# A post-norm decoder layer: the cross-attention's mask added by TensorE, weights by half blocks, last stages by halves

## The reference

```python
x = layernorm(x + self_attn(x))       # 32 heads of 16, qkv and output projections with biases
x = layernorm(x + cross_attn(x, ctx)) # q = x, k = v = ctx: 8 groups of 4 query heads, no projections
x = layernorm(x + ffn(x))
# cross_attn: scores = q @ k.T / 4 + mask[128, 128];  softmax(scores) @ v
# ffn: r = softmax(x @ gate_w.T)      # 8 experts
#      (x * (r @ in_scale)) @ sign(weight).T * (r @ out_scale) + bias
```

## Time and profile before

| | before |
|---|---|
| median of 3 runs | 362.21 us |
| profiled execution | 361.09 us |
| its span, first to last instruction | 359.2 us |
| mean granted TensorE clock | 0.979 |
| TensorE busy | 323.3 us (90%) |
| VectorE busy | 255.0 us (71%) |
| ScalarE busy | 190.0 us (53%) |
| GpSimd busy | 133.9 us (37%) |

### The profile page before, as it was taken

The page is one execution under the profiler, slowest core; times in us unless marked ns, Lnnn a source line. Parts: engine busy times, 40 slices in busy tenths (PEclk is TensorE's granted clock), DMA queues, the critical chain, the costliest instruction groups (busy, mean ns, idle before and its releaser), DMA issues.

```text
span 359.2 us, 7880 instructions
## 1 busy us (share of the span) xinstructions
PE 323.3 (90%) x2803; PEld 237.8 (66%) x2803; DVE 255.0 (71%) x828; ACT 190.0 (53%) x375; POOL 133.9 (37%) x217
## 2 busy tenths in 40 slices
PE   4997989897989999989999999999898997999992
PEld 3896866586765687767657698677475665754561
DVE  0693287135789955879999565989984778798646
ACT  2922733831148777531677865415689726536440
POOL 3352385973531124251472332423442243210311
PEclk9998999998999999999999999999999999899997
DMA  7946872454484012569451008982600045300001
GB/s 252 381 166 175 232 157 73 105 173 128 151 242 107 6 37 68 152 190 259 102 153 47 5 11 254 274 184 59 157 9 13 2 120 138 94 32 5 0 0 58
DMA packets 26119, 42.86 MB, mean 119 GB/s; under 512 B 7437, under 2 KB 17817, under 8 KB 23777
## 3 DMA queue, kind: packets, MB, share of 16 engines
q1 hardware_dynamic: 25769, 41.82, 41.5%
q10 hardware_dynamic: 312, 0.55, 0.4%
HBM read 29.58 MB, written 12.32 MB: 117 GB/s over the span
## 4 chain that ended last, share of the span: by engine, by line
PE 37%; DVE 34%; DMA 9%; issue 6%; SPq 4%; ACT 4%; POOL 4%; ACTq 0%; POOLq 0%; DVEq 0%
DVE x L948 7%; PE bank_a L1048 5%; DVE nma L865 4%; PE bank_a L1050 4%; PE bank_a L1049 4%; SPq L435 4%; PE bank_b L1233 3%; DMA out_dram<-x 3%; DVE wL L1017 2%; DMA ks<-scr_k 2%; DVE stb L829 2%; DVE x L965 2%; PE bank_a L1168 2%; PE bank_a L1137 2%; PE bank_a L1062 2%
## 5 line engine op out<-in xcount | busy, mean ns | idle before, releaser
L948 DVE CUSTOM_DVE_ANT_0 x<-bank_b,mraw 128x128 bf16<-128x128 f32 x192 | 42.3, 285 | 2.2 <-DMA out_dram<-x 1.5
L865 DVE TENSOR_REDUCE nma<-bank_a 128x4 f32<-128x512 f32 x64 | 40.0, 681 | 1.5 <-PE bank_a L1137 1.3
L741 ACT ACTIVATE pa<-bank_a 128x512 f32<-128x512 f32 x64 | 35.9, 598 | 8.7 <-PE bank_a L1154 6.8
L1048 PE MATMUL bank_a<-xH,wH 128*128 128x256 f32 x128 | 37.7, 294 | 0.7 <-DVE wL L1017 0.7
L1049 PE MATMUL bank_a<-xL,wH 128*128 128x256 f32 x128 | 36.5, 285 | 0.0
L1050 PE MATMUL bank_a<-xH,wL 128*128 128x256 f32 x128 | 36.5, 285 | 0.0
L606 POOL TENSOR_TENSOR qkp<-qr,qkp 128x512 bf16<-128x512 f32 x16 | 18.8, 1178 | 41.2 <-DVE qkp L861 41.2
L749 ACT ACTIVATE pb<-bank_b 128x512 f32<-128x512 f32 x54 | 29.9, 600 | 7.6 <-PE bank_b L1224 3.7
L712 ACT ACTIVATE qkp<-bank_a,bqk 128x256 bf16<-128x256 f32 x32 | 13.3, 471 | 33.9 <-PE bank_a L1050 23.8
L856 DVE SCALAR_TENSOR_TENSOR qr<-bank_a,bqk,qkp 128x256 f32<-128x256 f32 x32 | 14.0, 478 | 22.2 <-ACT qkp L712 22.1
L585 POOL TENSOR_SCALAR rsb<-mvb 128x1 f32<-128x1 f32 x16 | 3.7, 234 | 68.0 <-DVE mvb L831 68.0
(11 more groups left out here) (211 smaller groups left out, 808.4 us busy)
## 6 DMA issues: line engine op xcount, KB each, us to landing
wraw<-in_L_attn_attn_qkvw_dram SPq DMA_DIRECT2D x3, 1024.0 KB, 9.5
scr_q<-qkp SPq DMA_DIRECT2D x8, 384.0 KB, 3.0
qs<-scr_q SPq DMA_DIRECT2D x8, 384.0 KB, 4.5
scr_k<-qkp SPq DMA_DIRECT2D x8, 384.0 KB, 3.0
ks<-scr_k SPq DMA_DIRECT2D x8, 384.0 KB, 6.4
scr_x<-xp SPq DMA_DIRECT2D x8, 384.0 KB, 2.8
qx<-scr_x SPq DMA_DIRECT2D x8, 384.0 KB, 4.3
qs<-scr_q SPq DMA_DIRECT2D x8, 256.0 KB, 4.7
```

Source lines behind the costliest of these rows:

```text
L741: act.activation(pa[:, n % NP, :], pa_bank(i, *step)[:], ACT.Exp, scale=HD ** -0.5).then_inc(*ra.is_empty(i, *step))
L865: dve.tensor_reduce(nma[:, b, 4 * j:4 * j + 4], pa_bank(i, *step)[:].rearrange("p (m t) -> p m t", m=KT), AX.X, ALU.max, negate=True).then ...
L948: last = dve.tensor_tensor_reduce(unread[:, part * P:(part + 1) * P], pb_bank(i, *step)[:, r * P:(r + 1) * P], mraw[:], -1.0, -LOWEST, ALU ...
L1048: pe.matmul(dst, lh, rh, start=kt == 0, stop=False)
```

## The change

1. *Mask.* In every group TensorE adds the mask to `s`: two f32r products of 512 columns, the identity by the mask's high part and by its low part, laid down four times side by side. In group 3 it does the same for `st`, with mask and identity exchanged; the steps `sm`, and `sd` of group 3, are gone. In groups 0 to 2 `sd` stays with ScalarE. VectorE's maxima are the plain ones, one instruction a unit, in every group; x2 is no longer a scratch, and its wait for the stored output stands at `ot:b,0`. The raw mask lies in a part of `pa` until it is split.
2. *Weights.* The query block comes in four transfers; step `w` goes by five pieces, two halves of the query block, two of the key block, the value block; VectorE takes 2, 3, 3, 3 and 2 of the four tiles of each, GpSimd the others. A query or key step waits for its own pieces. The warming transposes before the first products change from 14, 8 and 30 to 0, 24 and 20, and x is transposed before the small operands.
3. *Router.* The exponentials are transposed as they are; the square of their sum's reciprocal is applied to the product's result, in the instruction that scales it. The scales are plain f32, 8 rows, and step `scales` is gone.
4. *Norm after the cross-attention.* After `ot:b,0` GpSimd adds the residual of the first 256 columns; VectorE takes the statistics of each half.
5. *Group 3's last stages.* `cx`, `is`, `ff`, `n2`, `n3` and the store go by halves of 256 columns.
6. *Buffers.* `rc` (context split) shares `xr` (x split), with waits between the two.
7. The table has an order of its own, and `UNREAD` 72 fillers in 21 places where it had 158 in 58.

```diff
@@ SyncE
-            sp.dma_start(wraw[:, :, 0:H], wv[:, :, 0:H]).then_inc(ld_w[0], 16)
+            for kt in range(KT):
+                sp.dma_start(wraw[:, kt, 0:H], wv[:, kt, 0:H]).then_inc(ld_wq[kt], 16)
...
@@ GpSimd
+                elif thread == "B" and name == "ot" and step[2] == 0:
...
+                    b = step[1]
+                    rb.wait_emptied(pool, i, *step)
+                    pool.tensor_tensor(by_head(x2[:, b, :])[:, 0:2], by_head(x2[:, b, :])[:, 0:2], tile_permuted(x1[:, b, :])[:, 0:2], ALU.add).then_inc(half_sum[b], 1)
...
@@ VectorE
+                    for k in range(GB):
+                        if earlier("ctx", k, place):
+                            dve.wait_ge(c_third[k], earlier("ctx", k, place))
                     rest = xr[:]
...
-                    if rb.has_mask(i, *step):
+                    if rb.has_mask(i, *step) or i in ADDED:
                         dve.tensor_reduce(nmb[:, b, :].rearrange("p (h k) -> p h k", k=KT)[:, 4 * (g % 2):4 * (g % 2) + 4, g // 2],
...
+                    if u == 1:
+                        dve.wait_ge(half_sum[b], 2 * i + 1)
+                        dve.bn_stats(stb[:, b, 0], x2[:, b, 0:HALF]).then_inc(half_sum[b], 1)
...
-                        dve.tensor_tensor(by_head(x2[:, b, :]), by_head(x2[:, b, :]), tile_permuted(x1[:, b, :]), ALU.add).then_inc(ln_b[b], 1)
-                        deviations(2 * i, x2[:, b, :], b)
+                        dve.tensor_tensor(by_head(x2[:, b, :])[:, 2:4], by_head(x2[:, b, :])[:, 2:4], tile_permuted(x1[:, b, :])[:, 2:4], ALU.add).then_inc(ln_b[b], 1)
+                        dve.wait_ge(ln_b[b], 6 * i + 1)
+                        dve.bn_stats(stb[:, b, 1], x2[:, b, HALF:]).then_inc(ln_b[b], 1)
+                        dve.wait_ge(half_sum[b], 2 * i + 2)
+                        aggregate(2 * i, b)
...
+                    dve.tensor_tensor(rl[:, b:b + 1], sl[:, b:b + 1], sl[:, b:b + 1], ALU.mult).then_inc(route_made[b], 1)
+                    dve.wait_ge(route_made[b], 2 * i + 1)
+                    dve.reciprocal(rl2[:, b:b + 1], rl[:, b:b + 1]).then_inc(route_made[b], 1)
...
+                    if i == LAST:
+                        h = step[2]
+                        part = slice(h * HALF, (h + 1) * HALF)
+                        rb.wait_full(dve, i, *step)
+                        dve.scalar_tensor_tensor(scaled[:, part], pb_bank(i, *step)[:, 0:HALF], rl2[:, b:b + 1], scaled[:, part],
+                                                 ALU.mult, ALU.mult).then_inc(*rb.is_empty(i, *step))
...
-                    for kt in range(KT if blk == 1 else WSPLIT):
+                    for kt in range(LOWS[piece]):
...
@@ TensorE
                     fresh = not rb.has_mask(i, *step)
+                    if fresh and i in ADDED:
+                        fresh = False
+                        if i == 0:
+                            pe.wait_ge(masks, 2)
+                        d4 = dst[:].rearrange("p (r t) -> p r t", r=4)
+                        for part in (mH, mL):
+                            pe.matmul(d4, idr[:], part[:].rearrange("p (o t) -> p o t", o=1).broadcast_to([P, 4, P]),
+                                      start=part is mH, stop=False, skip_group_check=True)
...
+                    if not rb.has_mask(i, *step):
...
+                        ident4 = idr[:].rearrange("p (o t) -> p o t", o=1).broadcast_to([P, 4, P])
+                        pe.matmul(d4, mH[:], ident4, start=True, stop=False, skip_group_check=True)
+                        pe.matmul(d4, mL[:], ident4, start=False, stop=False, skip_group_check=True)
...
-                    pe.wait_ge(route_made[b], i + 1)
-                    pe.transpose(dst[0:4 * E, 0:P], rts[:, b].rearrange("p k e -> p (k e)"), idf[:]).then_inc(*rb.is_full(i, *step))
+                    rb.wait_emptied(pe, i, "rt", b)
+                    pe.transpose(dst[0:E, 0:P], el[:, b, :], idf[:]).then_inc(*rb.is_full(i, *step))
...
@@ ORDER, start, before and after (group 3's end: cx, is, ff by halves)
-    C0.small A0.xt:0 A0.xt:1 C0.w:0 C0.w:1 A0.lc C0.w:2 A0.q:0 A0.q:1 A0.ldq:0 A0.q:2 A0.q:3 A0.ldq:1 A0.v:0 A0.ldk:0
+    C0.w:0 A0.xt:0 A0.xt:1 C0.small C0.vs A0.lc B0.cp:0 C0.w:1 C0.w:2 C0.w:3 C0.w:4 A0.q:0 A0.q:1 A0.ldq:0 A0.v:1
+    A0.q:2 A0.q:3 A0.ldk:0 A0.v:0 A1.xt:0 A1.xt:1 A0.ldk:1 A0.ldq:1 C0.ow B0.ctx:0 C0.mask A1.q:0 A1.q:1 A0.s:0,0
...
```

More of the change, by code:

```diff
@@ L58 @@
[L58 to L67, removed]
@@ L675, in _ @@
+                elif thread == "C" and name == "w":
+                    piece = step[1]
+                    for kt in range(LOWS[piece], KT):
+                        pool.wait_ge(w_high, KT * piece + kt + 1)
+                        low, raw = w_views(wL, wraw, kt, piece)
+                        pool.tensor_tensor(low, raw, high_view(kt, piece), ALU.subtract).then_inc(w_low_p, 1)
                 elif thread == "C" and name == "ow":
@@ L919, in _ @@
                         dve.wait_ge(c_third[1], i)
+                    for k in range(GB):
+                        if earlier("xt", k, place):
+                            dve.wait_ge(b_third[k], earlier("xt", k, place))
                     dve.tensor_tensor(rc[:], pb_bank(i, *step)[:, 0:P], cp[:, b, 0, :], ALU.subtract).then_inc(*rb.is_empty(i, *step))
@@ L1236, in _ @@
                     b = step[1]
-                    pe.wait_ge(x2_made[b], i + 1)
-                    for kt in range(KT):
-                        last = quarter(dst, kt, x2[:, b, kt * P:(kt + 1) * P])
+                    pe.wait_ge(x2_made[b], i + 1 + sum(step[2:]))
+                    for k, kt in enumerate(tiles_of(i, step)):
+                        last = quarter(dst, k, x2[:, b, kt * P:(kt + 1) * P])
                     last.then_inc(*rb.is_full(i, *step))
@@ L1259, in _ @@
                     rb.wait_emptied(pe, i, "rr", b)
-                    for kt in range(KT):
-                        last = pe.matmul(dst[:, kt * P:(kt + 1) * P], icS[:, kt * P:(kt + 1) * P], rT[:, tokens(b)], start=kt == 0, stop=kt == KT - 1,
+                    if i == 0 and b == 0:
+                        pe.wait_ge(ld_cs, 32)
+                    for k, kt in enumerate(tiles_of(i, step)):
+                        last = pe.matmul(dst[:, k * P:(k + 1) * P], icf[:, kt * P:(kt + 1) * P], rT[:, tokens(b)], start=k == 0, stop=True,
                                          skip_group_check=True)
@@ L1277, in _ @@
                     dst = pb_bank(i, "small")
-                    for _ in range(14):
-                        pe.transpose(dst[:, 0:P], idf[:], idf[:])
                     pe.wait_ge(ld_small, 48)
```

361 lines of the change are left out of this document (200 added, 161 removed), and 19 rows, old and new, of the table UNREAD.

## The result

The changed kernel takes 373.48 us (median of 4 runs, 370.54 to 377.0) against 362.17 (361.53 to 362.82) before: ratio 1.0285, 95% interval 1.0192 to 1.0378, so slower, and beyond the upper end of the range, 364 us. A second set of runs of the same kernel, beside the experiments, gave 374.7 us and 1.0346 (1.0292 to 1.0399), the whole interval more than 2% above the kernel before. Ratios leave out runs that are longer at a lower granted clock (one of the four above, two of ten of the f32r scales, 405.75 and 517.17 us, seven of ten of the mask's high part, one each of the last two kernels), while medians and ranges hold every run. here are those of the changed kernel unless another is named.

The account below looks back on a forecast made before the run. The middle alternates between TensorE and VectorE. Head -4.5, middle +2.0, last scores -3.3, last stages -4.6 sum to -10.4 from 361.09: 350.7, median 351.8, stated as 351.5 us; own range 345 to 358, 8-in-10 range 339 to 364.

Parts of the forecast that it names:

- Router and scales: Router: four small VectorE steps leave the last stages' path, 1.0 us; plain f32 scales no change, upper bound 1.7 us.
- third rival: Router's scale products: plain f32 takes four passes, 6.9 us, about 60% on the path, giving 356 us; chance 0.03.
- Mask in the middle: Groups 0 to 2: TensorE gets 22.5 us, 12.4 on the path; VectorE's shorter maxima give back 6.5 us.
- first rival: Middle: TensorE becomes the bound, 85% of the added 22.5 us on the path, giving 368 us; chance 0.19.
- Head: Kernel start: split weights, earlier x transposes and reordered reload bring first scores earlier, gain 4.5 us.
- head gain absorbed: Head's gain is lost before the cross-attention, by key 1 or the output projection's weights: 356 us; chance 0.12.
- Last group's scores: Group 3: TensorE adds the mask, 16 VectorE copies go; stretch from 24.8 to 21.5 us, gain 3.3.
- Last stages by halves: From the last values step to the end, 23.8 us: working by halves gains 4.6 us, between 2.5 and 6.
- Residual by halves: Groups 0 to 2: half the residual sum goes to GpSimd, gain 2.9 us; VectorE's added wait taken as 0.
- Scratch in x2 and shared buffers: Moved wait for the output's store: nothing, at most 0.44 us; shared split buffers: 0, up to 0.6 us in 8 places.

Follow-up runs that it names:

- the last two kernels: Both repairs, bf16 mask, last mask on VectorE, mask's step moved, 32-row f32r whole scales: 384.2 us; whole scales on both repairs and moved step only: 374.03 us.
- both repairs: Changed kernel with f32r scale products in one pass and only the mask's high part ahead of the maxima: 357.23 us, ratio 0.9837.

## Why the prediction was wrong

*Router and scales: the step that failed worst.* "I take no change, upper bound 0.11 x 16 = 1.7 us". With one f32r pass in its place the changed kernel takes 11.3 us less; plain f32 alone costs 6 to 7 in the old order. The reading was at fault: I held the time of one instruction of the plain f32 row against one f32r product. That row counts 8 for a step of four products, two instructions to a product, and I had the row in hand. The third rival had the mechanism, 6.9 us of TensorE and a chance of 0.03; measured are 9 at the full clock and 10.8 in all. The rule I had set aside holds: the Trainium skill ("FP8 and Floating Point Precision", TensorE Precision Notes) gives true FP32 four passes. The trace agrees: 1.05 us for 512 columns is 4.5 of the filler's slots of 0.234.

The other half of that step is four VectorE instructions that go from between the exponential and its transpose. I gave that 1.0 us, in the last stages only. In the kernel before, TensorE waited for them for 2.0 us over the whole span, four times, 0.8 the longest; in the changed kernel 0.2 us are left, for ScalarE's exponential. So this term was about right for the old order. Where two such instructions return to the new order, the wait is 11.4 us: the new order has no room for them. Rounding the weights once keeps that wait away without the price of plain f32, at the precision of one f32r pass.

*Mask in the middle.* "0.468 us by the filler's slot" was 0.55: the first product of a pair starts 0.314 us before the second, the second 0.238 before the scores, as the rows of one unit show:

```profile
266.08 0.48 PE L1272 MATMUL bank_b<-mH,idr 128*128 128x512 f32 x1
266.40 0.40 PE L1272 MATMUL bank_b<-mL,idr 128*128 128x512 f32 x1
266.64 0.40 PE L1275 MATMUL bank_b<-kx,qx 96*128 96x128 bf16 x4
266.84 0.48 PE L1272 MATMUL bank_b<-mH,idr 128*128 128x512 f32 x1
```

The filler's 0.234 was f32r behind f32r; behind bf16 scores the first costs 0.08 more. The unit is 0.76 us (266.08 to 266.84), not 0.69, while a plain maximum is the 0.60 I had. Over 48 units that is 4 us. The larger error is the net price: in the old order alone the move costs 14 us where I had 12.4 - 6.5 = 5.9. If VectorE gave back the 6.5, then 80% of TensorE's 26 us was on the path and not 55%; no run separates the two. The first rival ("TensorE becomes the bound", 0.19) was the case that came, and the time came out above its 368 us. The reason that I gave against it did not hold: I counted the run-outs of its bursts as room, and the second stretch shows 75.57 of 76 us busy. B0.s:0,0 to B2.st:1,7 grew by 11.3 us; with f32r scales it still grew by 7.4, with both repairs by 1.4.

*Head.* The first score was forecast near 44.5 and stands at 45.04: the weights' halves and the reordered reload did about what the sum said. Of these 4.0 us, 0.6 are left at A0.st:0,0 and 3.0 at B0.s:0,0, so "head gain absorbed" (0.12) came in small part, 1.5 us short of the sum's 4.5, and by another place than the two I named. What I didn't price is the splitting of the mask: its two VectorE instructions of 1.5 us stand in the new table ahead of group 1's query parts, and these ahead of the first maxima. The first maximum starts at 48.87, 0.6 us earlier than before; moving that one step won 3.7 us at B0.s:0,0 and 3.8 at the end. The eight fillers behind it (53.13, 2.11 us) held VectorE up once, for 1.25 us; no run prices them.

*Last group's scores.* I began the stretch a unit too early: 310.57 is the last unit of the first sequence, and the second's first is at 312.45, so before it was 22.9 us and not 24.8. After, it is 322.60 (the mask's first product) to 346.43, 23.8 us in place of 21.5. The eight score units take 6.0 for 5.5. A transposed unit behind another takes 0.70 (329.19 to 329.89), as in the sum, but one in front of a values step or a transpose about 0.88, so the sixteen are 11.9 for 11.0; the four values steps take 4.05 for 3.6, and the transposes, with a wait of 0.34 in the last, 1.8 for 1.4. No single term is far off: the 3.3 us of gain were 1.9 of the wrong start, and what is left was less than the 2.3 by which the terms were short.

*Last stages by halves.* Forecast -4.6 from the end of the last values step to the end (23.8 us before); measured 26.6, +2.8. With f32r scales it is 21.7 (340.11 to 361.82), -2.1: the right sign, and just under the 2.5 to 6 of the sum. The difference of 4.9 us is the plain f32 products and the lower clock, in the changed kernel's tail:

```profile
358.13 1.22 PE L1332 MATMUL bank_a<-rT,icf 8*128 8x128 f32 x4
359.14 1.06 PE L1332 MATMUL bank_b<-rT,icf 8*128 8x128 f32 x4
359.99 1.91 PE L1336 MATMUL bank_b<-ocf,rT 8*128 8x512 f32 x2
361.83 1.22 PE L1344 MATMUL bank_b<-swT,zH 128*128 128x256 f32 x4
```

3.7 us for one sequence's scales. The stretch around it, below the one before it:

```profile
348.00:356.00 8.00, 7.83 (x49) 4.63 (x47) 4.81 (x17) 2.90 (x11) 2.50 (x4) 1.00 0.01 2
356.00:366.00 10.00, 10.00 (x39) 8.01 (x39) 4.71 (x13) 2.17 (x5) 0.22 (x1) 0.52 0.00 1
```

The granted clock is 0.52, the lower of the two levels (1.2 of 2.4 GHz), after 8 us in which TensorE was busy for 7.83 at the full one. I took 0 for that and kept up to 4 us; TensorE is busy for all of these 10 us, so by my estimate, from the clock of 0.52 alone, up to 5 of them are the clock's. With f32r scales the granted clock from 341 us to the end is 0.91.

*Residual by halves.* VectorE waits for GpSimd's half three times, 3.0 us, 1.0 the longest, within what the range held for it:

```profile
DVE stb L988 <- POOL x L657: 3.0, 3, 1.0
```

*Scratch in x2 and shared buffers* leave no wait in the lists of the changed kernel worth a term.

In one sum, by stretches of the profile against the forecast's -10.4: the head -3.0 for -4.5; from B0.s:0,0 to B3.st:1,7, which is the middle and most of the last scores, +15.1 for -1.3; from there to the end +1.7 for -4.6. By causes, undone one on top of the other: 374.7 us, 363.44 with f32r scales (11.3 less), 357.23 with the mask's high part alone (6.2 less), 353.41 with the mask's step moved (3.8 less). What the mask's move costs in the new order no run isolates; in the old one it is 14 us. With three small edits the kernel takes 3.0% less than before, at one f32r pass for the scales and the rounded mask under the maxima. That this is 2 us from the forecast is luck: the forecast had both mask products, and its terms for the middle, the last scores and the last stages are off one by one.

## What to carry to other kernels

Count instructions per product before you price a type: a group's count over its steps shows when the engine splits a product in two, and a mean per instruction hides it. Work moved to an engine that is over 90% busy can be on the path for most of its price, whatever engine leads the chain before: here 14 us stayed of 26, after what the other engine was spared. And a gain at the head of a kernel can end at the first engine whose own queue has something else in front: read that queue, in order, up to the instruction that takes the gain over.

## What the runs showed of the hardware

- A plain f32 product of 512 columns holds TensorE for 0.95 to 1.05 us at the full clock, by what follows it, as two instructions, with 8 rows or 32; one f32r pass over 32 rows mostly took 0.37 to 0.43, over 128 rows, behind another f32r product, 0.23.
- An f32r product right behind bf16 ones starts its successor 0.08 us later than behind f32r (0.314 and 0.238 for the same shape); a bf16 product of the same shape starts its successor after 0.22.
- A 128x128 cast on VectorE took 1.57 us at 42.50, and the same cast 0.22 us at 56.60 in the kernel with the step moved; the context's cast took 1.18 us at 41.40, and 0.23 in the kernel before at 40.63. Beside the two long ones GpSimd was busy throughout (1.50 of 1.50 us in each window), beside the two short ones it was idle (0.00 and 0.06 of 1.00 us). The reloads alone don't explain it: the DMA share was 0.77 at the short cast at 40.63. No run varies GpSimd by itself, so the cause stays open.
- Taking work off TensorE made this kernel slower: 386.48 us with the mask's sum back on VectorE, with a granted clock of 0.926 over the span against 0.969.
